# Query projections in four column tiles, a later value-bias spread and an earlier first xT load in a cross-attention kernel

## What is computed

```
Q = relu(x @ Wq + bq);  K = relu(ctx @ Wk + bk);  V = relu(ctx @ Wv + bv)
scores = einsum('hbqd,hbkd->hbqk', Qh, Kh) * scale      # 16 heads of 8 features
attn = softmax(scores masked by empty key rows) * (query row not empty)
out = einsum('hbqk,hbkd->hbqd', attn, Vh) + x
```

## Time and profile before

| | |
|---|---|
| median of three runs | 355.8 us |
| profiled execution, its own time | 355.79 us |
| its span, first to last instruction | 354.1 us |
| mean granted TensorE clock | 0.996 |
| PE busy | 345.4 us (98%) |
| ACT busy | 299.4 us (85%) |
| DVE busy | 236.4 us (67%) |
| share of PE in the chain that ended last | 94% |

### The profile page before, as it was taken

How to read it: one execution, slowest core, us unless ns; L and a number is a source line. 1 busy time by engine, 2 the same in 40 slices (tenths; PEclk the granted TensorE clock), 3 DMA queues, 4 the chain that set the end, 5 groups by cost and what they waited for, 6 DMA issues and landing times.

```text
span 354.1 us, 16749 instructions
## 1 busy us (share of the span) xinstructions
PE 345.4 (98%) x6698; PEld 235.4 (66%) x6698; DVE 236.4 (67%) x777; ACT 299.4 (85%) x395; POOL 4.4 (1%) x28
## 2 busy tenths in 40 slices
PE   7999999999999999999999999999999999999994
PEld 4665676776757677675767767576676767667662
DVE  4789487775848577484867848486784848679321
ACT  1587789888898988889898898989889898989993
POOL 4000000000000000000000000000000000000000
PEclk9999999999999999999999999999999999999998
DMA  7578657777954746384464738447473754537100
GB/s 253 199 256 294 208 189 240 262 228 203 318 136 179 217 149 224 91 292 135 175 201 159 234 91 290 138 169 211 151 239 91 281 149 169 179 109 240 11 10 8
DMA packets 41667, 65.29 MB, mean 184 GB/s; under 512 B 28197, under 2 KB 30758, under 8 KB 41638
## 3 DMA queue, kind: packets, MB, share of 16 engines
q1 hardware_dynamic: 40420, 64.09, 56.2%
q10 hardware_dynamic: 1218, 0.79, 0.8%
HBM read 13.67 MB, written 0.82 MB: 41 GB/s over the span
## 4 chain that ended last, share of the span: by engine, by line
PE 94%; DVE 2%; DMA 2%; issue 1%; ACTq 1%; ACT 0%
PE psum L694 40%; PE psum L670 29%; PE psum L614 12%; PE psum L605 11%; DMA query_rep<-in_xT 2%; PE psum L785 1%; DVE values L951 1%; ACT probs L568 0%; DVE k_low L922 0%; DVE v_biased L941 0%; ACTq L514 0%; ACTq L516 0%; ACTq L518 0%; PE psum L793 0%; DVE flat_mask L1109 0%
## 5 line engine op out<-in xcount | busy, mean ns | idle before, releaser
L568 ACT ACTIVATE probs<-psum 121x800 f32<-121x800 f32 x384 | 293.3, 840 | 37.5 <-PE psum L670 37.5
L694 PE MATMUL psum<-probs,values 121*17 121x200 f32 x3072 | 154.8, 334 | 0.0
L670 PEld LDWEIGHTS psum<-query_bd,k_parts 64*121 64x121 f32 x1536 | 91.7, 181 | 50.8 <-ACT probs L568 35.0
L670 PE MATMUL psum<-query_bd,k_parts 64*121 64x200 f32 x1536 | 115.5, 281 | 0.3 <-ACT probs L568 0.2
L694 PEld LDWEIGHTS psum<-probs,values 121*17 121x17 f32 x3072 | 78.0, 97 | 41.3 <-issue 1.7
L898 DVE TENSOR_SCALAR_CACHE_REDUCE k_raw<-psum,bk_sb 128x361 f32<-128x361 f32 (+2 forms) x63 | 37.3, 593 | 53.9 <-PE psum L605 53.8
L614 PE MATMUL psum<-wv_sb,keyT 128*32 128x129 f32 (+1 forms) x1536 | 53.8, 273 | 0.1
L605 PE MATMUL psum<-keyT,wk_mixed 128*32 128x361 f32 (+2 forms) x504 | 51.3, 481 | 1.2 <-DVE flat_mask L1109 0.6
L614 PEld LDWEIGHTS psum<-wv_sb,keyT 128*32 128x32 f32 (+1 forms) x1536 | 43.7, 108 | 6.4 <-DVE v_biased L941 0.5
L951 DVE TENSOR_SCALAR values<-v_biased,keep 121x128 f32<-121x128 f32 x192 | 43.3, 283 | 6.1
L941 DVE TENSOR_TENSOR v_biased<-psum,bv_sb 121x384 f32<-121x384 f32 x64 | 35.0, 548 | 0.0
(11 more groups left out here) (77 smaller groups left out, 64.0 us busy)
## 6 DMA issues: line engine op xcount, KB each, us to landing
k_parts<-k_high SPq DMA_DIRECT2D x30, 722.0 KB, 4.8
k_parts<-k_low SPq DMA_DIRECT2D x30, 722.0 KB, 5.4
keyT<-in_ctxT SPq DMA_DIRECT2D x15, 722.0 KB, 4.2
query_rep<-late_high SPq DMA_DIRECT2D x2, 600.0 KB, 3.8
query_rep<-late_low SPq DMA_DIRECT2D x2, 600.0 KB, 4.2
residual<-in_x SPq DMA_DIRECT2D x64, 12.5 KB
out<-residual SPq DMA_DIRECT2D x60, 12.5 KB
k_parts<-k_high SPq DMA_DIRECT2D x2, 359.0 KB, 3.4
```

Source lines behind the costliest of these rows:

```text
L568: nc.scalar.activation(probs[0:KTILE, u % PROB_SLOTS], scores_ps[0:KTILE, u % SCORE_SLOTS, :, 0:QCOLS], ACT.Exp, scale=SCALE).then_inc(pro ...
L670: mm = nc.tensor.matmul(scores_ps[0:KTILE, u % SCORE_SLOTS, j, n * TCOLS:(n + 1) * TCOLS], k_parts[rows, parity, t, kt * KTILE:(kt + 1) * ...
L694: mm = nc.tensor.matmul(spans[c * VCOLS:c * VCOLS + VUSED, half, :, :, 0:SPAN], values[0:KTILE, parity, kt, half * HALF_PAIRS + c, 0:VUSED ...
```

## The change

Three edits. The first-xT load moves ahead of `bq` and Wq on ACT's queue. Each query projection is made of four products with 32 columns of the weights each, written to 32 partitions of the bank each. The spread of the value bias with its two waits moves from right behind the first projection to right ahead of `select_first_queries`.

```diff
             act.dma_start(bk_sb[:], bk.rearrange("(t i) o -> i t o", t=QUADS), allow_slow_non_contiguous=True
                           ).then_inc(bk_loaded, 16)
+            act.dma_start(xT_sb[:, 0].rearrange("p (b q) -> p b q", b=QB), xT[:, 0:QB, :]
+                          ).then_inc(first_xT_loaded, 16)
             act.dma_start(bq_sb[:], bq.rearrange("(t i) o -> i t o", t=QUADS), allow_slow_non_contiguous=True
                           ).then_inc(bq_loaded, 16)
             act.dma_start(wq_sb[:], Wq).then_inc(wq_loaded, 16)
-            act.dma_start(xT_sb[:, 0].rearrange("p (b q) -> p b q", b=QB), xT[:, 0:QB, :]
-                          ).then_inc(first_xT_loaded, 16)
...
             def project_queries(g, bank):
-                return nc.tensor.matmul(bank[:, 0:QB * SQ], wq_mixed[:], xT_sb[:, g], start=True, stop=True)
+                for m in range(0, P, VCOLS):
+                    mm = nc.tensor.matmul(bank[m:m + VCOLS, 0:QB * SQ], wq_mixed[:, m:m + VCOLS], xT_sb[:, g],
+                                          start=True, stop=True)
+                return mm
+
+            def spread_value_bias():
+
+                pe.wait_ge(bv_loaded, 16)
+                pe.wait_ge(first_evacuated, 1)
+                nc.tensor.matmul(psum[:, BV_BANK, 0:D], ones[0:1, :], bv_row[:], start=True, stop=True).then_inc(bv_spread, 1)
...
             project_queries(0, psum[:, Q_BANKS[0], :]).then_inc(q_projected, 1)
-            pe.wait_ge(bv_loaded, 16)
-            pe.wait_ge(first_evacuated, 1)
-            nc.tensor.matmul(psum[:, BV_BANK, 0:D], ones[0:1, :], bv_row[:], start=True, stop=True).then_inc(bv_spread, 1)
...
             for g in range(VGROUPS):
                 if g == VGROUPS // 2:
+                    spread_value_bias()
                     select_first_queries()
```

## The result

The changed kernel takes 359.0 us (median of six runs, 358.13 to 361.52) against 355.5 for the kernel before beside it (six runs, 354.74 to 355.85). The ratio is 1.0109, with a 95% interval of 1.0089 to 1.0128: 1.1% slower. The forecast was 354.8, the range ended at 356.0, and slower had a chance of 0.06. The profiled execution of the changed kernel is its slowest, 361.52 us with a span of 359.8.

A forecast was written before the change was run, and what follows sets the result against it. TensorE was taken to bound the kernel, so its first 35 us decide. Savings of 0.69 + 0.17 + 0 + 0.17 = 1.03 us, from 355.80, gave 354.8 us; the range ran from 354.2 to 356.0.

The forecast's parts named there:

- First xT earlier: Start, ACT's queue: xT issued at 1.96 instead of 3.25 lands at 6.8 to 7.3, before TensorE can use it at 8.35.
- Wq's landing: Start, ACT's queue: Wq, now last, lands at 7.9, bounds 6.7 and 9.0 or 9.13; VectorE wants it at 7.53.
- The rule of the Trainium skill that I weighed: DMA engines alternate between queues packet by packet: Wq would land near 9.13 and the time be 356.0 us.
- The price of a late Wq: VectorE ahead of key chunks 1 and 2: stopped d = 0.4 us by Wq, paid from 0.78 us of room.
- The rival with the other sign: Wq so late that VectorE's stop at mix_columns eats the gain: 355.2 to 356.0 us; chance 0.22, 0.06 for slower by over 0.2%.
- gain = 1.09 - d: Start of the selecting products: gain in us with VectorE stopped d, capped by TensorE's 10.91; 0.69 expected, from 11.97 to 11.28.
- The idle time to be won: TensorE between key projections (end 8.35) and first query projection (9.27): 0.92 us idle, ended by xT, open to be gained.
- The bias spread: Ahead of the selecting products: its 0.41 us falls where TensorE waits for q_split anyway, so it costs nothing.
- Four column tiles: Query projections: 0.17 us saved each, bounds 0.06 and 0.28; second and fourth count 0.17 each, the first within its 0.70.
- The third projection: At 16.88: saves nothing, since the scores behind it wait 0.17 us longer for ScalarE's third exponential.
- I charge nothing: First scores and reads of values: low-key copies land by 13.6, scores start at 14.5; no loss of lead charged.
- The lead passes on: 60 to 200 us: TensorE, busy 140.00 of 140.00 us, passes on any lead or lag from the start one for one.

The follow-up runs named there:

- e10_sp_later: Changed kernel with SP's two large loads issued only when key chunk 1 has landed, just after Wq's issue; 355.38 us, ratio 0.9997.
- e11_rest_sooner: Kernel before with SP's 600 KB load of the later xT issued ahead of bv, and so ahead of the first xT; 358.74 us, ratio 1.0085.
- e1_old_order: Changed kernel with the loads of bq, Wq and first xT back in their old order; 355.11 us, ratio 0.9988.
- e8_bq_last: Changed kernel with Wq issued ahead of bq on ACT's queue (first xT, Wq, bq); 355.54 us, ratio 1.0002.
- e5_filled: Changed kernel with 14 unread products of ones ahead of TensorE's wait for the reordered Wq; 358.32 us, ratio 1.0075.
- e16: Changed kernel with the old order of loads and all four first key copies issued by SP, none by ACT; 355.89 us, ratio 1.0003.
- e3_wq_first: Changed kernel with Wq issued ahead of the first xT and bq last on ACT's queue; 355.44 us, ratio 0.9997.
- e4: Changed kernel with Wq issued by SP between key chunks 0 and 2, no longer on ACT's queue; 355.64 us, ratio 0.9999.
- e7: Changed kernel with SP issuing its 600 KB and 722 KB loads only when Wq has landed; 356.4 us, ratio 1.0022.
- e15_copies_held: Changed kernel with SP's large loads after key chunk 1's landing and its second key copies held until the first four landed; 358.93 us, ratio 1.0070.
- e12: Kernel before with nothing but the query projections in four column tiles; 355.12 us, ratio 1.0005.

## Why the prediction was wrong

**First xT earlier.** Right: landing in 6.8 to 7.3, measured 7.27, and no idle time of TensorE put down to it.

**Wq's landing: the step that failed.** I took 7.9, with 9.13 as the upper bound; it was 10.2. "The queue serves its transfers in the order of issue" looked at ACT's queue alone. The bulk of xT ended near its place, but Wq then didn't start: SP's 600 KB, issued 0.08 us before it (3.10 against 3.18), were served first. e10_sp_later and e11_rest_sooner show it in both directions. The upper bound was the landing of the transfer that had stood last before, and that one was issued level with SP's load, not behind it. I had left SP's queue out of the sum. The reorder shifted it too: bv's issue took 0.34 us in place of the 0.51 it takes with the old order (e1_old_order), which brought SP's load forward from 3.26 to 3.10, just as Wq was moved back from 2.61 to 3.18.

The rule of the Trainium skill that I weighed (DMA: Bandwidth & Descriptors, Queues, rings and completion order) has each DMA engine take turns between its queues packet by packet, and I had made 9.13 of it. The measured 10.2 lies beyond that too. The page's packet is a bundle of up to 64 descriptors, though, and I had counted turns in the profile's small packets. In those the queues did not alternate: in e8_bq_last SP's went first. Whether turns in larger bundles would give the measured times no run here shows.

**The price of a late Wq.** The rival with the other sign named the place, `mix_columns` on VectorE, and the rule gain = 1.09 - d. VectorE took up Wq at 10.25 in place of 7.53, so d is 2.72 and the selecting products should come at 11.97 + 1.63 = 13.60. In e5_filled, at full clock, they came at 13.61. The rule held, far outside the d that I had allowed. What it lacked is TensorE's own wait: 3.16 us of idling, and behind it up to 10 us at 1.2 GHz, so that TensorE's own chain put them at 14.51 and the first scores another 2.8 us further back. My text priced a stall of TensorE at its length.

**The idle time to be won.** The 0.92 us of one trace came back as 0.91, 0.78 and 0.67 in three others with the old order, and as nothing in a fourth. It is the distance between two times that move from execution to execution: xT landed at 9.13 in the trace that I had and at 8.0 to 8.2 in the others, and the keys were through at 8.35 there, at 8.24 in e16 and at 7.4 in the rest. The prediction took both for fixed.

**The bias spread.** No cost relative to before, as predicted, by 2.70 against 2.70 us. That it would be covered by a wait did not come up: in the changed kernel TensorE never waited for `late_low`. In e5_filled, e3_wq_first and e8_bq_last it waits 0.40, 0.53 and 0.81 us there, and the spread is hidden.

**Four column tiles.** Right in size: 0.70 us ahead of the value products, 0.79 ahead of the scores, near 0.2 saved per pair. The third projection gave most of its saving back to the scores behind it, as the prediction had it. The time doesn't show the rest: 1.0005, with an interval that holds both nothing and the 0.34 us claimed.

**"I charge nothing" for the copies of the low keys.** Wrong, though hidden by the larger error. In the traces of e3, e4, e7, e8 and e10, with xT early and Wq in time, these copies, the first or the second set, take back what TensorE had gained. For the first set that is read from the landing times, since the releaser named is another. Had Wq landed in time, the forecast of 354.8 would still have been too low: such versions (e3, e4, e8, e10) gave 355.4 to 355.6, with ratios of 0.9997 to 1.0002.

**The lead passes on.** Right, for a lag: 5.65 us at 38 us, 5.7 at the end.

No version beats the kernel before beyond its interval. The best is e1_old_order, the tiles and the spread with the old order of issues, at 0.9988 (0.9973 to 1.0004).

## What to carry to other kernels

Before a small load that something waits for is moved back by half a microsecond, lay the issue times of all queues side by side: what counts is which large load it falls behind, on its own queue or on another. Price a new wait of TensorE by its length and by the clock afterwards. And take an idle time, and the two times that it lies between, from more than one execution before it is put down as a gain, and name the next transfer that the earlier engine will meet.

## What the runs showed of the hardware

- A small transfer issued just behind another engine's large one was served mostly after it: 64 KB landed in 3.6 to 4.6 us issued 0.5 us and more ahead of another queue's 600 KB, in 5.3 issued 0.10 ahead, and in 7.0 to 7.3 issued 0.08 us behind it. Half a kilobyte, issued level with it, took 6.4 to 6.6 us.
- After 3.2 us without work TensorE's granted clock went to 0.50 while it was busy again. How long it stayed differed between executions of one kernel: mean clocks of 0.986 to 0.999, times of 361.5 to 358.1. Fourteen products of ones kept it at 1.00. It also fell behind waits of 1.83 us (e7_sp_waits) and 1.70 us (e15_copies_held).
- The time of an issue itself differed with what stood around it: bv's took 0.34 us with the new order on ACT's queue and 0.51 with the old one. That moved SP's load from 3.26 to 3.10, ahead of Wq's 3.18.
- The 24 key products took 2.63 us in some executions and 3.60 in others (e1, e12 and the changed kernel; the kernel before), while the clock rows read 1.00 in both. Why stays open.
